# Spreading the maximum products of a 1444-key attention evenly over its key tiles, and turning the maxima one key tile later

## What is computed

```python
qm = _split_heads(q @ Wq.T + bq)
km = _split_heads(k @ Wk.T + bk)
vm = _split_heads(v @ Wv.T + bv)
scores = jnp.einsum('bnlh,bnph->bnlp', qm, km) / np.sqrt(HEAD_DIM)
scores = jnp.where(mask, scores, MASK_FILL)
attn = jax.nn.softmax(scores, axis=-1)
out = jnp.einsum('bnlp,bnph->bnlh', attn, vm)
```

## Time and profile before

| | |
|---|---|
| median of 3 runs | 2269.28 us |
| lowest, highest | 2267.26, 2281.24 us |
| span of the profiled execution | 2267.4 us |
| stage B in the trace | first score product at 595.9 us, last at 1727.9 us |

### The profile page before, as it was taken

The page is one execution under the profiler, slowest core; times in us unless marked ns, Lnnn a source line. Parts: engine busy times, 40 slices in busy tenths (PEclk is TensorE's granted clock), DMA queues, the critical chain, the costliest instruction groups (busy, mean ns, idle before and its releaser), DMA issues. The chain is left out here.

```text
span 2267.4 us, 43146 instructions
## 1 busy us (share of the span) xinstructions
PE 1969.0 (87%) x16922; PEld 1258.0 (55%) x16922; DVE 1578.2 (70%) x3726; ACT 1324.7 (58%) x2169; POOL 551.4 (24%) x477
## 2 busy tenths in 40 slices
PE   3679999667999999999999999999997888888997
PEld 2546666444556556565565655556564555555554
DVE  4845666795787877878788788878771566664554
ACT  3645776683366666666666666666664555553444
POOL 1411322314122212222221222222222132311122
PEclk9879999777799999999999999999998788788999
DMA  5025554012132323233131322313222001103441
GB/s 153 1 92 183 184 173 142 4 37 91 65 109 74 126 68 118 78 105 119 68 126 63 120 85 101 121 66 122 79 89 67 16 8 16 31 1 59 67 71 40
DMA packets 120023, 189.26 MB, mean 83 GB/s; under 512 B 36770, under 2 KB 94090, under 8 KB 118414
## 3 DMA queue, kind: packets, MB, share of 16 engines
q1 hardware_dynamic: 119822, 186.50, 26.6%
HBM read 103.33 MB, written 11.76 MB: 51 GB/s over the span
## 5 line engine op out<-in xcount | busy, mean ns | idle before, releaser
L1610 DVE TENSOR_REDUCE b_part_max<-psum 128x1 f32<-128x482 f32 (+3 forms) x1248 | 737.6, 651 | 188.1 <-PE psum L1487 174.1
L1400 ACT ACTIVATE b_PT<-psum 128x800 f32<-128x800 f32 x768 | 616.6, 836 | 386.1 <-PE psum L1506 381.1
L1487 PE MATMUL psum<-b_KH,b_QBD 64*128 64x482 f32 (+1 forms) x1152 | 422.6, 445 | 45.7 <-DVE b_part_max L1610 43.3
L1506 PE MATMUL psum<-b_QS,b_KS 64*128 64x200 f32 x3072 | 438.3, 288 | 0.5 <-ACT b_PT L1400 0.3
L1506 PEld LDWEIGHTS psum<-b_QS,b_KS 64*128 64x128 f32 x3072 | 339.4, 186 | 16.2 <-issue 11.8
L1522 PE MATMUL psum<-b_PT,b_V 128*32 128x200 f32 x6144 | 341.4, 339 | 0.6 <-ACT b_PT L1400 0.6
L1487 PEld LDWEIGHTS psum<-b_KH,b_QBD 64*128 64x128 f32 x1152 | 197.3, 189 | 198.6 <-DVE b_part_max L1610 118.4
L1322 POOL TENSOR_TENSOR b_KL<-b_KF,b_KH 128x1444 fp32r<-128x1444 f32 x32 | 106.8, 3338 | 693.3 <-PE psum L1506 670.1
L1522 PEld LDWEIGHTS psum<-b_PT,b_V 128*32 128x32 f32 x6144 | 159.9, 109 | 149.1 <-ACT b_PT L1400 82.3
L1900 ACT ACTIVATE c_HE<-psum,C 128x400 f32<-128x400 f32 x128 | 75.7, 595 | 94.6 <-PE psum L2116 90.1
L1474 PE MATMUL psum<-W,b_CT 128*128 128x128 f32 (+1 forms) x768 | 117.7, 293 | 12.6 <-DVE b_part_max L1610 6.7
(11 more groups left out here) (280 smaller groups left out, 3095.2 us busy)
## 6 DMA issues: line engine op xcount, KB each, us to landing
b_KS<-b_KH SPq DMA_DIRECT2D x64, 722.0 KB
a_CT<-in_ctxt SPq DMA_DIRECT2D x32, 722.0 KB, 5.5
b_CT<-in_ctxt SPq DMA_DIRECT2D x32, 722.0 KB, 4.4
b_KS<-b_KL SPq DMA_DIRECT2D x32, 722.0 KB
a_CN<-in_ctxn SPq DMA_DIRECT2D x32, 704.0 KB
att_scratch<-b_AO SPq DMA_DIRECT2D x32, 200.0 KB, 1.9
c_G<-gates_scratch SPq DMA_DIRECT2D x4, 1600.0 KB
c_KBD<-gates_scratch SPq DMA_DIRECT2D x4, 1600.0 KB
```

The source lines that it names most:

```text
L1400: nc.scalar.activation(PT[:, kt % 2, 2 * a:2 * a + 2, :], psum[:, 2 * a:2 * a + 2, 0:TG], ACT.Exp).then_inc(sem["pt_ready"], 1)
L1487: m = mm(bank(b, D, size), QBD[rows, j % 2, tile * D:(tile + 1) * D], KH[rows, j % 2, at_:at_ + size], start=True, stop=True)
L1506: m = mm(bank(p, D, 2 * T, (s % 2) * 2 * T), KS[rows, j % 2, s, kt * D:(kt + 1) * D], QS[rows, j % 2, s * 2 * T:(s + 1) * 2 * T], start=Tr ...
L1610: v.tensor_reduce(part_max[0:rows, q, c:c + 1], bank(b, rows, CHUNKS[c][1]), AX.X, ALU.max)\
```

## The change

`MAIN_TILES` is computed: every key tile holds three maximum products, two upper and one lower in even key tiles, one upper and two lower in odd ones, again starting with key tile 9. `EARLY` becomes 9. The last of the 36 now lies in key tile 8, behind the three left ones, so `mx` is reduced after it (`LAST_MAX`), and the turn moves from phase 4 of key tile 8 to phase 4 of key tile 9. Since the next element's first products follow soon, DVE waits for its own `mx` before the first of them.

```diff
-MAIN_TILES = ((9, 2, 2), (10, 2, 2), (11, 2, 2), (0, 2, 2), (1, 2, 1), (2, 1, 2), (3, 2, 1), (4, 1, 2), (5, 2, 1), (6, 1, 2), (7, 1, 1))
+MAIN_TILES = tuple((kt % KT, 2 - kt % 2, 1 + kt % 2) for kt in range(9, 9 + KT))
...
+LAST_MAX = len(MAINS) - 1
...
-        jobs.append(((g, j + 1, "turn", 0), PHASES * 8 + 4))
+        jobs.append(((g, j + 1, "turn", 0), PHASES * 9 + 4))
...
-    for i in range(MAXES):
+    for i in range(LAST_MAX):
         jobs.append((0, 0, "max", i))
-        if i % 12 == 3 and i < len(MAINS):
+        if i % 12 == 3:
             jobs.append((0, 0, "value", i // 12))
+    jobs += [(0, 0, "max", len(MAINS) + c) for c in range(3)] + [(0, 0, "max", LAST_MAX)]
     jobs.append((0, 0, "turn", 0))
...
                 elif kind == "max":
                     half, tile, c = max_tile(i)
+                    if i == 0:
+                        wait(dve, sem["mx_ready"], n)
...
-                    if i == MAXES - 1:
+                    if i == LAST_MAX:
                         dve.wait_ge(drained, done)
                         v.tensor_reduce(mx[:, 0:QCH], part_max[:, :, :], AX.X, ALU.max, negate=True).then_inc(sem["mx_ready"], 1)
```

## The result

The changed kernel takes 2370.32 us (median of 4 runs, 2351.79 to 2376.27) against 2271.7 for the kernel before on the same chip: ratio 1.0413, 95% interval 1.0361 to 1.0465. It is slower, as forecast, but by some 100 us instead of 40, and outside the range of 2285 to 2352.

The account below looks back on a forecast made before the run. PE was taken to bound stage B, half the span. Slot changes of +1.37 us over 31 slots gave +42.5, less 1.8 before the first slot: 2308.1 from the 2267.4 span, 2310 us as median; range 2285 to 2352.

Parts of the forecast that it names:

- the wait and its size: Key tile 11: PE waits 1.80 us at the next element's first score for the turn's late DMAs; tile +1.19.
- The landing: Last of the turn's four small DMAs: rows in place 1.5 us after its issue starts, between 1.1 and 1.9.
- the sign: Waits view: new PE or PEld entry at line 1506, about 1.4 to 1.8 us, 31 times, ended by a DMA into `QS`.
- the tiles: Stage B slot, key tiles: 7 and 8 +0.58 us each, 9 -0.31, 10 -0.26, 0 -0.41, 11 +1.19.
- the sum: Stage B: key tile changes add to +1.37 us a slot, +42.5 us over 31 slots, the clock costed at nothing.
- Forecast 2310, with a chance of 0.60: Whole kernel: 2310 us, its own range 2295 to 2325, with the late rows' wait but no clock cost.
- the rival: PE's wait also drops the clock in stage B: 26 us for half the elements, 2336; in all, 2361; chance 0.20.
- those rows: Stage C, 3.3 us windows: clock fell to 0.50 after 1.93 us of PE busy, stayed 1.00 after 2.21.
- The argument against: Against a falling clock: PE nearly full around the wait, idle under 1.5 us by the last product's modelled end.
- On SP's queue the loads for later elements stand behind the four DMAs; they are due a slot later.: SP's queue at the turn: loads behind the small DMAs are due a slot later; no cost put in.
- the evening out wins: Rows in place within 4.35 us of key tile 9's start: no wait, slot 0.23 us faster, total 2260; chance 0.06.

Follow-up runs that it names:

- The run that shows rows and spread alone: Changed kernel with the tokens' load issued ahead of the small DMAs and two unused 256-column products in PE's wait: 2304.39 us, ratio 1.0129.
- the late turn without the spread: Kernel before with only the turn moved one key tile later, products left as they lay: 2326.82 us, ratio 1.0211.

## Why the prediction was right or wrong

*Right: the wait and its size.* Counted from the start of key tile 9, by the timeline above: `NMH` and `NML` done and SP's first issue at 2.84 (forecast 2.93), last issue at 4.56 (4.65), PE at key tile 11 at 4.42 (4.35), first score at 6.11 (6.15). The landing, taken as 1.5 after the last issue between bounds of 1.1 and 1.9, allowed the score 1.55 after it. The waits view shows 1.2 and not the 1.4 to 1.8 that were to be the sign: PE enters the tile 1.69 before the score, but it runs the product ahead of the wait, 0.48, in that time. The Trainium skill, page "DMA: Bandwidth & Descriptors", section "Anatomy of one DMA", gives its fixed cost of 2.0 us for DMAs that GpSimd issues; here SyncE issues them, and 2.0 would have been 0.45 too long.

*Right: the tiles.* Key tile 7 takes 3.62 and 8 takes 3.05, as worked out by the tiles of equal content; 9 and 10 take 2.26 and 2.16 instead of 2.15 and 2.20; 11 takes 3.56 instead of 3.65; 0 takes 1.89 instead of 2.05 where no query stands in it. The late rows and the spread together, 1170.5 - 1134.3 = 36 us of stage B, answer to the 42.5 that the sum gave for 31 slots. That they come so close is partly luck: the late rows cost 53.3 us, where the sum has 1.60 in each slot, 50, and the spread with the rows in place gains 17.1, where it has 7. With the rows in place key tiles 11 and 0 took 1.90, not 2.05. The run that shows rows and spread alone was 1.3 per cent above the kernel before; the forecast was 1.8.

*Wrong: "Forecast 2310, with a chance of 0.60", in which the clock holds, against 0.20 for the rival.* This is the step that failed first. The mechanism was named, its place was right, and the earlier trace rows showed both outcomes; but the idling was weighed as lying between them and then given to the harmless side, so the sum has the clock at nothing. The reading was kind, too: a wait of 1.80 is longer than PE's idling in either of those rows (1.37 where the clock fell, 1.09 where it held), and lies between them only once the product ahead of the wait is taken off. The argument against, that the idle would be under 1.5, was true (1.2) and no help: without the tokens in the way, the clock still fell after 18 of the 31 waits. That cost 37 us by itself, between the rival's own 26 for half of the elements and 51 for all.

*Wrong: "On SP's queue the loads for later elements stand behind the four DMAs; they are due a slot later."* That holds for the context vectors and masks: no wait of PE for them shows. The tokens of the group after next are issued in a group's last slot and are used at key tile 0 directly after it. This is how it was before, in the slot of the earlier trace rows:

```profile
1027.07 0.43 SPq L1221 DMA_DIRECT2D b_HT<-h3t_scratch  x1
...
1034.00 1.63 PE L1455 MATMUL psum<-b_HT,W 128*128 128x136 f32 x6
```

No wait shows at the projection. Moved behind a later turn, with PE arriving where it did, the load came up to 4.6 us late. This was not in the sum and not among the rivals. It cost 20 us in stage B, with the clock that it takes along.

Together 57.7 us in stage B, less the 6 by which rows and spread came out cheaper than the sum; that is 51 of the miss of 60, as far as one profile of each kernel tells. The other 9 lie outside stage B, where the profiles differ by more than that. The rival "the evening out wins" was right in its sign and its condition: with the rows in place, the spread gains.

*The range* reached 2352 for a clock that falls in most elements. It lacked the tokens, and one run of four lies at its edge.

## What to carry to other kernels

When an instruction that feeds a DMA is moved later in an engine's list, follow everything queued behind that DMA on its issuing queue to its first user, one by one; a load that seems a slot away may be due a few microseconds later. Where TensorE bounds the loop, a wait in each pass, here of little over 1 us in some 37, should be priced twice, once for the time and once for the clock, and a filler of useless matmuls is the cheap experiment that tells the two apart. A tile's cost after a change is well read off a tile of today with the same content.

## What was not expected of the hardware

How little more idling made the difference. Of 30 waits of 0.8 us at the score (the late turn without the spread) none brought the clock down without a wait for the tokens beside it; of 31 waits of 1.2 us or more, with the tokens' wait taken out, 18 did, and the mean clock of stage B was 0.96. The two kernels also differ in the work around the wait, so no run shows that the length alone decides. After one and the same amount of PE work in 3.3 us, 2.10, the clock fell in one slot and held in another. The runs of the changed kernel differ by 24 us (2351.79 to 2376.27), and the fastest has the highest mean clock (0.905), the slowest the lowest (0.892). The Trainium skill, page "TensorE: Matmul & The Clock Gate", section "HAM oscillation", has this mechanism with longer waits as its example; here waits of 1.2 us were enough in many elements.
